# Joining the half-filled passes of two key tiles in the large cross-attention stages

## The reference, cut to what matters

```
stage 0  self   16 heads x 64     stage 4  cross  16 heads x 64
stage 1  cross  16 heads x 64     stage 5  self   16 heads x 16, masks
stage 2  self   16 heads x 64     stage 6  cross  16 heads x 16, mask
stage 3  cross  16 heads x 64
```

```
q = (layernorm(x) @ Wq)                 112 x 1024
k = (ctx @ Wk), v = (ctx @ Wv)          375 x 1024, contraction over 192
x = x + softmax(q k^T * scale) v @ Wo + bo     per head of 64
```

## Time and profile before

| | us |
|---|---|
| median of 3 runs | 1679.66 (1677.42 to 1682.25) |
| the profiled execution, its own time | 1679.83 |
| its span, first to last instruction | 1678.0 |
| TensorE busy in the span | 1599.0 |
| VectorE / ScalarE / GpSimd busy | 1036.2 / 1011.4 / 794.8 |

### The profile page before, as it was taken

One profiled execution on the slowest core, in us unless ns is written; L12 is line 12 of the kernel. 1 busy time (PEld: TensorE's weight loads), 2 busy tenths in 40 slices (PEclk: granted clock), 3 DMA queues, 4 the chain that ended last, 5 costly groups with the idle time before them and its releaser, 6 DMA issues.

```text
span 1678.0 us, 38143 instructions
## 1 busy us (share of the span) xinstructions
PE 1599.0 (95%) x14070; PEld 1390.6 (83%) x14070; DVE 1036.2 (62%) x2706; ACT 1011.4 (60%) x2877; POOL 794.8 (47%) x1316
## 2 busy tenths in 40 slices
PE   7999999999989999999999989999999988899988
PEld 6888888888888888888888888888888777777768
DVE  7756565556566655665555566765556468766774
ACT  6666656666624556666666633566656676677771
POOL 3554366566432444356666431466656413334320
PEclk9999999999999999999999999999999989999999
DMA  5323200001111101200001110100001100101000
GB/s 161 100 86 110 68 15 15 15 19 50 59 35 38 42 2 39 74 22 15 15 15 49 56 43 26 56 18 15 16 29 39 64 18 4 32 17 31 18 2 23
DMA packets 37879, 65.14 MB, mean 39 GB/s; under 512 B 6784, under 2 KB 12384, under 8 KB 37696
## 3 DMA queue, kind: packets, MB, share of 16 engines
q1 hardware_dynamic: 37120, 62.65, 11.8%
q10 hardware_dynamic: 576, 0.05, 0.0%
HBM read 57.15 MB, written 5.54 MB: 37 GB/s over the span
## 4 chain that ended last, share of the span: by engine, by line
PE 82%; DVE 8%; ACT 4%; issue 4%; POOL 2%; DMA 1%; ACTq 0%; DVEq 0%
PE pG L1113 49%; PE pG L1265 12%; PE pO L1113 10%; PE pS L1113 10%; ACT P L1435 1%; DVE KF L1575 1%; DVE x L1618 1%; ACT PT L1448 1%; POOL P L1699 1%; DVE bn L1492 1%; DVE whole_f L1530 1%; DVE tmp L1616 1%; DVE nmax L1557 1%; DVE full L1638 0%; PE pG L1318 0%
## 5 line engine op out<-in xcount | busy, mean ns | idle before, releaser
L1699 POOL TENSOR_SCALAR P<-P,rinv 112x375 f32<-112x375 f32 (+1 forms) x640 | 330.7, 529 | 289.5 <-DVE rinv L1581 287.6
L1435 ACT ACTIVATE P<-pS,nmax 112x375 f32<-112x375 f32 (+1 forms) x640 | 306.4, 491 | 197.6 <-DVE nmax L1557 197.4
L1113 PE MATMUL pG<-hT_hi,W 128*128 128x224 f32 (+1 forms) x1408 | 321.5, 308 | 18.1 <-POOL hT_lo L1753 4.9
L1557 DVE TENSOR_REDUCE nmax<-pS 112x1 f32<-112x375 f32 (+1 forms) x448 | 229.9, 548 | 63.1 <-PE pS L1113 62.4
L1113 PEld LDWEIGHTS pG<-hT_hi,W 128*128 128x128 f32 x1408 | 241.9, 194 | 30.1 <-issue 6.3
L1448 ACT ACTIVATE PT<-pG 125x336 f32<-125x336 f32 (+1 forms) x448 | 207.0, 467 | 94.3 <-PE pG L1265 92.6
L1265 PE MATMUL pG<-ident,P 112*125 112x112 f32 (+1 forms) x1472 | 239.9, 277 | 12.4 <-POOL P L1699 6.7
L1113 PE MATMUL pG<-src,W 128*128 128x376 f32 x1120 | 242.1, 346 | 0.3 <-DVE hid_hi_f L1525 0.3
L1265 PEld LDWEIGHTS pG<-ident,P 112*125 112x125 f32 (+1 forms) x1472 | 199.5, 176 | 48.8 <-issue 6.1
L1113 PE MATMUL pG<-W,src 128*125 128x512 f32 x840 | 235.0, 412 | 3.0 <-ACT whole_f L1390 1.9
L1113 PE MATMUL pG<-hT_lo,W 128*128 128x224 f32 (+1 forms) x704 | 209.8, 298 | 0.0
(11 more groups left out here) (120 smaller groups left out, 2834.0 us busy)
## 6 DMA issues: line engine op xcount, KB each, us to landing
wraw<-wts SPq DMA_DIRECT2D x110, 256.0 KB, 2.6
src<-ctx_split SPq DMA_DIRECT2D x64, 282.0 KB, 3.0
ctx_split<-hid_lo_t SPq DMA_DIRECT2D x8, 564.0 KB, 3.6
whole_f<-wts SPq DMA_DIRECT2D x14, 256.0 KB, 6.3
V<-ctxT SPq DMA_DIRECT2D x8, 376.0 KB, 4.3
bo_b<-bo SPq DMA_DIRECT2D x10, 112.0 KB, 3.0
out<-x SPq DMA_DIRECT2D x8, 112.0 KB, 1.9
x<-x_in SPq DMA_DIRECT2D x1, 672.0 KB, 10.4
```

What stands on the lines that cost most here:

```text
L1113: return nc.tensor.matmul(o, l, r, start=first, stop=last)
L1435: ins = act.activation(o, pS[U % 4][0:T, i * n:(i + 1) * n], ACT.Exp, bias=nmax[:, r, i:i + 1], accum_out=rsum[:, r, i:i + 1])
L1557: dve.tensor_reduce(nmax[:, r, 0:sh.G], ps, AX.X, ALU.max, negate=True).then_inc(maxed, 1)
L1699: ins = pool.tensor_scalar(o, o, rinv[:, r, i:i + 1], st.nscale, ALU.mult, ALU.mult)
```

## The change

For the slots of batches 0 to 6 in stages 1, 3 and 4 (which make the keys of batches 1 to 7, `joined`), that is 3 x 28 slots of two key tiles each:

1. A key tile runs only its first four passes and leaves its bank open. A new item `kk` then runs the last pass of both tiles with 64 contraction rows each: tile 2i in the upper row half of the array, tile 2i+1 in the lower, each into its own bank.
2. For the lower half the 64 context rows must stand in partitions 64 to 127 as hi: a new buffer `src_half`, loaded by one more DMA per context batch (64 partitions x 376 x 4 bytes = 96 KB). It lies over `maskf`, and the first mask waits for the last `kk` of stage 4.
3. The two key tiles move to the end of the slot: first, second of them with the last transpose between, then `kk`, and then the next slot's `set`. Queries and the other work of the slot alternate in front of them.
4. The even tile of each pair is evicted by ScalarE (`by_act`), the odd one by VectorE as before.
5. `AHEAD` of queries and values goes from 1.5 to 2.5: they come sooner in ScalarE's queue, in every stage.

```diff
+def joined(s, b):
+    return s in (1, 3, 4) and 0 < b < B
+def by_act(e):
+    return e.kind == "k" and joined(e.s, e.b) and e.i % 2 == 0
...
+        if joined(d.s, d.b + 1):
+            keys = [Ev("k", d.s, d.b + 1, 2 * d.i + j) for j in range(2)]
+            qs, rest = [e for e in early if e.kind == "q"], [e for e in early if e.kind != "q"]
+            early = [e for pair in zip_longest(qs, rest) for e in pair if e]
+            order += (between(early, scored[:-1], 0, 1) if scored else early) + keys[:1] + scored[-1:] + keys[1:]
+            order.append(Ev("kk", d.s, d.b + 1, 2 * d.i))
+        else:
+            order += (between(early, scored, 0) if scored else early) + work[len(early):]
...
-AHEAD = dict(ta=1.5, tb=1.5, ql=1.5, q=1.5, v=1.5, k=1.5, qk=1.5, lnt=1.5, wo=1.5, ff2=1.5, ffg=1.5, ffa=1.5, raw=1.5, trans=2.5, ao=2.0, hn=.5)
+AHEAD = dict(ta=1.5, tb=1.5, ql=1.5, q=2.5, v=2.5, k=1.5, qk=1.5, lnt=1.5, wo=1.5, ff2=1.5, ffg=1.5, ffa=1.5, raw=1.5, trans=2.5, ao=2.0, hn=.5)
...
+                    if joined(s, b):
+                        sp.dma_start(src_half[64:128, n % 2, :].bitcast(F32), ctx_split[b, 0:64, 2 * SP:3 * SP]).then_inc(src_in[n % 2], 16)
...
-                    accumulate(g[:, 0:SP],
-                               [(wv[0][0], c[0]), (wv[0][0], c[1]), (wv[0][1], c[0]), (wv[1][0], c[2]), (wv[1][1], c[2])]
-                               ).then_inc(pieces, 1)
+                    passes = [(wv[0][0], c[0]), (wv[0][0], c[1]), (wv[0][1], c[0]), (wv[1][0], c[2])]
+                    if joined(s, b):
+                        for n, (l, r) in enumerate(passes):
+                            mm(g[:, 0:SP], l, r, n == 0, False)
+                    else:
+                        accumulate(g[:, 0:SP], passes + [(wv[1][1], c[2])]).then_inc(pieces, 1)
+                elif e.kind == "kk":
+                    n = NCROSS[s, b]
+                    slot, col, ks = st.k
+                    for t in range(2):
+                        rows = slice(64 * t, 64 * t + 64)
+                        lo = w_view(slot, 1, col + ks + (e.i + t) * 128, 128)[rows]
+                        c = src_half[rows, n % 2, :] if t else src[rows, n % 2, 2 * SP:3 * SP]
+                        ins = mm(g_bank(Ev("k", s, b, e.i + t))[:, 0:SP], lo, c, False, True)
+                    ins.then_inc(pieces, 2)
...
+                elif e.kind == "k":
+                    wait(act, scored, keys_free(s, b, e.i))
+                    if split(s, b):
+                        rest_free(act, s)
+                    o = keys_rest(e.i, whole_f) if split(s, b) else KF[:, e.i, 0:SP]
+                    act.activation(o, g[:, 0:SP], ACT.Copy).then_inc(ka_ready, 1)
...
+                    if m == 0:
+                        wait(pool, pieces, piece_no[Ev("k", 4, B - 1, 7)])
```

More of the change, by code:

```diff
@@ L2 @@
 from contextlib import ExitStack
+from itertools import zip_longest
 import numpy as np
@@ L242, in fill @@
         if not last:
[L243 to L246, removed]
+            if odd:
+                out += [Ev("q", s, pr + 1, t) for t in (2 * i, 2 * i + 1)]
         if i == 0 and b == 0 and opened:
@@ L305, in fill, with between @@
     return out
-def between(work, turned, first):
+def between(work, turned, first, more=0):
     out = []
-    at = [first + n * (len(work) - first) // len(turned) for n in range(len(turned))]
+    at = [first + n * (len(work) - first + more) // len(turned) for n in range(len(turned))]
     for i in range(len(work) + 1):
@@ L337, in tensor_order @@
         early = work[:ffs[1]] if len(ffs) > 1 else work
-        order += (between(early, scored, 0) if scored else early) + work[len(early):]
+        if joined(d.s, d.b + 1):
[6 more added lines that the diff above has]
+            order += (between(early, scored, 0) if scored else early) + work[len(early):]
         scored = [Ev("trans", d.s, d.b, u) for u in SHAPES[d.s].units(d.i)]
@@ L409, in duration @@
             return .75 if st.small else 2.83
-        return dict(ta=.48, tb=.27, q=.68, qk=1.36, k=.86, lnt=.23, ffg=1.24, ffa=1.24, ff2=2.83)[k]
+        return dict(ta=.48, tb=.27, q=.68, qk=1.36, k=.69 if joined(e.s, e.b) else .86, kk=.26, lnt=.23, ffg=1.24, ffa=1.24, ff2=2.83)[k]
     if engine == "act":
@@ L425, in duration @@
             return 2.7 + .5 * len(GELUS[e.s][e.i])
-        return dict(tb=.74, qk=.76, w=.6, q=.35, ffg=.62, ctx=.9, lnt=.45)[k]
+        return dict(tb=.74, qk=.76, w=.6, q=.35, ffg=.62, ctx=.9, lnt=.45, k=.5)[k]
     if engine == "dve":
@@ L466, in task, with made @@
         ready_at[engine, e] = not_before
+    def made(e):
+        return "pe", Ev("kk", e.s, e.b, e.i // 2 * 2) if e.kind == "k" and joined(e.s, e.b) else e
     def evicted(e):
@@ L471, in evicted @@
             return "dve", e._replace(kind="ql")
-        if e.kind in ("q", "v"):
+        if e.kind in ("q", "v") or by_act(e):
             return "act", e
@@ L543, in plan @@
                 else:
-                    needs += [("dve", Ev("ql", s, b // 2, t)) if s == 6 or split(s, b) else ("act", Ev("q", s, b // 2, t)), ("pool" if s == 6 or split(s, b) else "dve", Ev("k", s, b, t))]
+                    needs += [("dve", Ev("ql", s, b // 2, t)) if s == 6 or split(s, b) else ("act", Ev("q", s, b // 2, t)), ("pool", Ev("k", s, b, t)) if s == 6 or split(s, b) else evicted(Ev("k", s, b, t))]
             needs += [read(unit_no(s, b, u) - 4) for u in us if unit_no(s, b, u) > 3]
@@ L561, in plan @@
         elif e.kind == "k" and (s == 6 or split(s, b)):
-            task("dve", e, ("pe", e))
-            task("pool", e, ("dve", e))
+            task(*evicted(e), made(e))
+            task("pool", e, evicted(e))
         elif e.kind in ("qk", "k"):
-            task(*evicted(e), ("pe", e))
+            task(*evicted(e), made(e))
         elif e.kind in ("wo", "ff2", "ta"):
@@ L666, in plan @@
         task("sp", Ev("mask", s, b), ("dve", Ev("scores", s0, b0, SHAPES[s0].NU - 1)))
-        task("pool", Ev("mask", s, b), ("sp", Ev("mask", s, b)))
+        task("pool", Ev("mask", s, b), ("sp", Ev("mask", s, b)), ("pe", Ev("kk", 4, B - 1, 6)) if m == 0 else None)
     for b in range(B):
@@ L738, in program @@
     k_no = number(order["dve"], "k", "qk")
+    ka_no = number(order["act"], "k")
     qk0_no = number([e for e in order["act"] if e.s == 0], "qk")
@@ L805, in program @@
         src = sb("src", [128, 2, 3 * SP], F32R)
+        place = nc.sbuf_base
+        maskf = sb("maskf", [T, 2, SP])
+        src_half = nc.alloc_sbuf_tensor_at("src_half", [128, 2, SP], F32R, offset=place)
         craw = V[:, 2, 0:2 * SP].rearrange("p (k n) -> p k n", k=2)
@@ L811, in program @@
         mask_words = sb("mask_words", [T, 2, SP // 4], I32)
-        maskf = sb("maskf", [T, 2, SP])
         lo_rows_sb = sb("lo_rows_sb", [128, 1])
@@ L860, in program @@
         ao_rounded, ao_split = sem("ao_rounded"), sem("ao_split")
-        q_ready, k_ready = sem("q_ready"), sem("k_ready")
+        q_ready, k_ready, ka_ready = sem("q_ready"), sem("k_ready"), sem("ka_ready")
         v_ready = sem("v_ready")
@@ L1031, in heads_of, with src_count @@
             return view.rearrange("p (h d) -> p h d", d=32)[:, :, 16 * part:16 * part + 16]
+        def src_count(n):
+            return 16 * sum(2 + joined(*key) for key, m in NCROSS.items() if m <= n and m % 2 == n % 2)
         def ring(key):
@@ L1135, in work_start @@
                         pe.wait_ge(qk5_ready, qk5_no[f])
+                    elif f in ka_no:
+                        pe.wait_ge(ka_ready, ka_no[f])
                     elif f.kind in ("k", "qk"):
@@ L1189, in _ @@
                     n = NCROSS[s, b]
-                    wait(pe, src_in[n % 2], 32 * (n // 2 + 1))
+                    wait(pe, src_in[n % 2], src_count(n))
                     slot, col, ks = st.k
@@ L1232, in _ @@
                                     wait(pe, k_split, split_no[Ev("k", s, b, t)])
+                                elif Ev("k", s, b, t) in ka_no:
+                                    wait(pe, ka_ready, ka_no[Ev("k", s, b, t)])
                                 else:
@@ L1712, in _ @@
                     n = split_no[e]
-                    pool.wait_ge(k_ready, k_no[e])
+                    if e in ka_no:
+                        pool.wait_ge(ka_ready, ka_no[e])
+                    else:
+                        pool.wait_ge(k_ready, k_no[e])
                     if s < 6:
```

## The result

The changed kernel takes 1662.97 us (median of 4, 1660.74 to 1664.35) against 1679.97 us: a ratio of 0.9898, 95% interval 0.9878 to 0.9918, or 17.0 us with 13.8 to 20.5 us as bounds. A second series on another occasion gave 0.9881 (0.9863 to 0.9899), which would be 1660 here. The forecast was 1667.5, 12.3 us: the direction was right, and 1662.97 lies in the forecast case (1661 to 1673), near its edge, while the second series falls just outside. The gain was a third larger than forecast; even the lower bound, 13.8 us, is above the forecast.

The account below looks back on a forecast made before the run. TensorE's instruction stream was taken to bound the changed stretches. Removed passes -28.6, joint passes +14.3 and order +2 gave -12.3 us, with evictions and the rest at zero: 1667.5 us from 1679.8, range 1658 to 1679.

Parts of the forecast that it names:

- forecast case: Whole kernel: a measured time of 1661 to 1673 us, given 0.58.
- What bounds the kernel: Stretches of changed slots, 782 us: TensorE's instruction stream sets the time, so a removed pass is worth its pace.
- What a pass is worth: Key tiles: a last pass is worth 0.17 us; 168 removed passes give 28.6 us.
- The term of 14.3 us: Changed slots: net gain, 28.6 us for removed passes less 14.3 us for the joint passes.
- What the joint pass costs: `kk` before each `set`: one pair at 0.17 us, the entry into halves only moved; 14.3 us over 84 slots.
- The first rival: `kk` and `set`: the joint pass drains twice, 14.3 us more, 1682 us; given 0.20 together with half the gain eaten.
- Evictions: Key tiles: 84 evictions moved to ScalarE, about 42 us of its work, cost zero time.
- The order of values and queries: Values-first slots, keys last: bank waits partly remain, about 2 us given back; bounds -10 and +35 us.
- the two terms: Each changed slot: passes removed less joint pass, a gain of 0.17 us per slot.
- The second rival: Transposes or key tiles waiting for value or query banks: ScalarE's queue becomes the bound, 1691 us at 0.3 per slot; 0.08.
- The third rival: Bank waits of values and queries: today's losses go too, up to 10 us more gain, 1656 us; 0.14.
- The signs that were named: Stretches shrink 8 to 18 us, other stages move at most 3; also tile, pair and slot times, and TensorE waits.

Follow-up runs that it names:

- experiments 1: Changed kernel, but the last passes of both key tiles run over all 128 rows, one after the other: 1674.59 us, 0.9963 of the kernel before.
- experiment 3: Changed kernel, but both half-filled passes use the upper row half: 1677.22 us, 0.9981 of the kernel before.
- experiment 2: Changed kernel, but the joint pass stands in front of the slot's last transposes: 1689.79 us, 1.0065 of the kernel before.
- experiment 4: Changed kernel, but VectorE evicts both key tiles as before: 1662.52 us, 0.9896 of the kernel before.
- experiment 7: Changed kernel, but VectorE evicts both key tiles for keys of batch 1 and the first two pairs of batch 7: 1658.51 us, 0.9869.
- experiment 5: Changed kernel with the old queue priorities of values and queries (1.5): 1682.28 us, 1.0013 of the kernel before.

## Why the prediction was right, and where not

**What bounds the kernel**: right. TensorE's stream sets the stretches; 16.4 of 17 us came there.

**What a pass is worth** (0.17): right, 0.14 to 0.19 us in nearly every steady slot, 0.16 in the median (experiments 1 and 3). The term of 14.3 us was mis-sized by the count: it measured 10.3 to 11.9 us, since eight of the 84 slots gain nothing, three of them seen to wait for ScalarE's exponentials instead.

**What the joint pass costs** (one pair, entry shared): right. The first rival, the drain paid twice, is refuted by the scores' first pair of 0.16 to 0.17 us and the 0.28 us from the joint pass to the scores. The rule of the Trainium skill cited there ("TensorEngine Tiling (Array Packing)", Key Properties) agrees with experiment 2, where the pair stands among full-array work. The price in the prediction was too low: 0.17 was given for the middle of full-array work, 0.35 was measured.

**Evictions** (zero): right as a sum (experiment 4), wrong as "zero in each slot". In the second slot of batch 6 in stages 3 and 4, a key eviction now stands ahead of an exponential that the scores wait for: 8.87 us, where the kernel before took 8.06. Giving those evictions back to VectorE brought 8.39 and 8.11 (experiment 7).

**The order of values and queries** is the step that failed, in sign: "Together about **2 us** given back". Measured with the joint pass taken away, order, priorities and evictions together gain 6.3 us. Of the slots that were to lose, the second even ones lost nothing: from 8.05 to 7.89 is just the 0.17 of the two terms. The odd ones lost nothing either, but for some 0.1 us in their fourth slots (8.91 to 8.81). The first even ones won 0.54 beside the 0.17, not 0.35. The reason given for the loss (V behind a transposed tile in ScalarE's queue) was the right one; its cure was judged too weakly. The sum moved only the second V ahead of one tile, 0.35 us, and took the exponential ahead of it for a loss that stays. But the first V of the slot moved as well, into time in which ScalarE had stood idle, so that the exponential came 0.42 us sooner and V 0.88 us. One reading was wrong too: the 0.16 us of waiting lie inside the 1.26 between 830.07 and 831.33 and were not to be added; 0.32 us were lost there, and the rest of the 0.55 in the distances around it.

That 12.3 us came near the 17 is in part luck: the joint pass brought 2 to 4 us less than its 14.3, and the order 8 us more than its -2.

**The second rival**, ScalarE's queue as the bound, is what experiment 5 shows: at up to 0.7 us a slot the values-first order eats all of the joint pass. The priority is not an addition worth 5.5 us, as it is in the old order, but 17 to 19 us in the new one. **The third rival** ("the losses of today go too", 1656, given 0.14) came about in most of the steady slots.

**The signs that were named.** The three stretches shrank by 16.4 us, within 8 to 18. The stretches around them changed by 2.4, -0.8, -1.4 and 0.8 us, none by more than 3. Four-pass tiles take 0.76 (0.77 expected), and the first pair 0.16 to 0.17 instead of 0.26. TensorE's waits for V and queries add up to 3.2 us over the three stretches, under the 5 that would have shown the second rival. The slot lengths are the sign that missed: 7.90 in place of 8.0 to 8.1 and of 8.1 to 8.2.

## What to carry to other kernels

Two half-filled passes joined in the row halves are worth one pass, if they stand beside work that uses the same halves; a place one item away costs more than the pass. When items that share banks change their order, the queue of the engine that evicts them must change with them: here a missed turn cost some 0.6 us, more than three times the pass gained (0.17). Test such parts together as well as apart: without the joint pass the change gained 6 us, without the priorities it lost 2, the priorities alone gained 6, and all of it gained 17.

## What the runs showed of the hardware

A pair of half-array matmuls between full-array groups cost 0.35 us over one beside other half-array work, and part of it (0.51 against 0.25 us) appeared in the transposes behind it, which now stood between two such groups. With two passes in the upper half and none in the lower, the lower half ran two matmuls ahead of the upper, and a score matmul (765.97) started before a pass that the program issues ahead of it (766.23, experiment 3). Two executions of one program reached stage 1 3.4 us apart, at mean granted clocks of 0.91 and 0.97 of full speed over the first 60 us.
